# The last turn of a two-layer graph kernel re-ordered, its padding cleared by GpSimd, and the mean of the last normalization taken off by TensorE

## The chip, the core and the metric

The kernel runs on one core of a Trainium2 chip. The metric is device time in microseconds (us), the median of three executions. The core has five engines with a queue each: TensorE (PE in the rows; its weight loads are PEld), VectorE (DVE), ScalarE (ACT), GpSimd (POOL) and SyncE (SP), which here only issues DMAs. They wait for each other by semaphores: an instruction counts one up when it ends, another waits until the count is reached.

## The reference

There are N = 12,500 nodes with D = 32 features and E = 400,000 edges, sorted by destination. Two message layers follow one another, each with a normalization behind it. Cut to what matters:

```
m = relu(x[src] + edge_attr)
x = layernorm(x + (1 + eps) * x + segment_sum(m, dst))

out_deg = clip(segment_sum(1, src), 1);  in_deg = clip(segment_sum(1, dst), 1)
agg = segment_sum((x * rsqrt(out_deg))[src], dst)
x = layernorm(x + agg * rsqrt(in_deg))
```

`layernorm` takes the mean of a node's 32 features off and divides by the square root of the variance plus 1e-5. Everything is float32 (f32).

## The kernel before

**Layer 0** (`layer_0`, lines 221 to 689) goes through the edges in G = 125 groups of 3,200, as 128 partitions by J = 25 edges. Each engine has a function `step(g, slot, u)` that is its share of turn g, and `turns` calls it for g = 0 to 126. In turn g the kernel gathers the feature rows of group g (GpSimd, 25 indirect DMAs, line 163), sums the messages of group g-1, adds what was summed for group g-2 to the accumulator `acc`, and builds counts of group g for layer 1 (TensorE `built`, ScalarE evicts them to `big`, SyncE stores `big` to `stash` in HBM). Turn 125, which the change touches, has no group left to gather or build: it only sums the messages of group 124. Turn 126 only adds the last sums.

What VectorE does for the messages of one group, in halves of 13 and 12 edges: `add(h)` (line 422, waits for the gathered `rows` and for ScalarE's copy of the edge features, L589), `left(h)` (427) and `last_part(h)` (431), between which ScalarE rounds two bf16 parts (596, 600). These three parts of a message go into `msg`. `copy(1)` of ScalarE waits for `last_part(0)`, since both halves use the one bank `sum_ps`. Beside this VectorE makes `indices()` (lines 435 to 440) and from them the one-hots that TensorE multiplies by: `dst_hot`, `hi_hot` and `lo_hot` (all but the last from the helper in line 143, `lo_hot` in line 452). TensorE's 25 matmuls `agg<-hot,msg` (line 663) need all of it: the first 13 wait for the one-hots and the parts of half 0, the other 12 for those of half 1. Once they are done, lines 473 and 474 take the sums out of the bank (`taken`, `degree`).

At the end of layer 0 the buffer `big`, which held counts for `stash`, is used anew: its front becomes `x_0`, the node features. In turn 125 VectorE waits until all stores to `stash` have landed, clears 32 padded partitions (line 470) and counts `z_clear` up. SyncE waits for that and issues the loads of `x_0` (lines 546 and 548).

**finish_0** (lines 1005 to 1173) normalizes after layer 0. It transposes `acc` tile by tile (line 1051), and its first use of `x_0` is line 1060, behind the wait in line 1105. A chain of small DMAs runs beside it: the degrees go to HBM (line 1162) and come back turned (1164, 1165), and line 1114 waits for them. **layer_1** (694 to 900) then multiplies the stored counts by the node table.

**finish_1** (lines 1175 to 1277) is the last stage. The 98 columns of nodes that each partition holds are worked on in 7 chunks of 14 (`FR`), and these in two parts: part 0 has 4 chunks (56 columns, 1,792 elements for each partition), part 1 has 3 (42 columns, 1,344 elements). TensorE turns `acc`, which has features on partitions, into node-major tiles: 98 transposes of 32x128, 14 to a PSUM bank, over four banks. VectorE does `normed(k)` for a chunk (scaling by `r_in`, line 1212), then for a part `mean(h)` (add the residual, reduce, scale: lines 1218, 1220, 1222), `centred(h)` (subtract, 1227), `variance(h)` (1232) and `result(h)` (reciprocal 1237, multiply 1239). ScalarE squares (1259) and takes the root (1261). SyncE stores a part when `result(h)` is done.

`general_sums` is a fallback whose loops are skipped for these inputs; only its branches run. Engines meet at a barrier where one block of the program ends and the next begins.

Of the kernel before, what the change touches and what calls it, by code (L numbers as in the profile page):

```python
# [5 lines left out]
ALU = mybir.AluOpType  # L6
# [3 lines left out]
P = 128  # L10
# [6 lines left out]
def build(nc, x, src, dst, edge, eps, out, table, x1):  # L17
# [47 lines left out]
    with ExitStack() as ctx:  # L65
# [16 lines left out]
        fold = sb("fold", [D3, D])  # L82
        fold_r = sb("fold_r", [R, DE])
# [95 lines left out]
        with nc.Block() as block:  # L179
# [7 lines left out]
            def _(ve):  # L187
# [21 lines left out]
                ve.wait_ge(s_v, n)  # L209
                V(ve.tensor_scalar(fold[:, :], iota[0:D3, 0:D], low[0:D3, 0:1], None, ALU.is_equal))  # L210
# [10 lines left out]
        def layer_0():  # L221
# [37 lines left out]
            with ExitStack() as own:  # L259
# [133 lines left out]
                with nc.Block() as block:  # L393
                    @block.vector
                    def _(ve):
# [16 lines left out]
                        def step(g, slot, u):  # L412
# [47 lines left out]
                            if sends(g):  # L460
                                add(0)
                            if builds(g):
                                chunk(g, k, 1)
                            if sends(g):
                                left(0)
                                indices()
                            if isinstance(g, int) and g == G:
                                for k in range(2):
                                    ve.wait_ge(z_stash[k], (NC + 1 - k) // 2 * 16)
                                ve.memset(x_0[P - 32:P, TAIL:C, :], 0.0).then_inc(z_clear, 1)  # L470
                            if adds(g):
                                ve.wait_ge(z_agg, g - 1)
                                ve.tensor_copy(taken[:, :], agg).then_inc(z_taken, 1)
                                ve.tensor_tensor(degree[:, :], degree[:, :], agg_degree, ALU.add).then_inc(z_degree, 1)
                            if builds(g):
                                chunk(g, k, 2)
                            if sends(g):
                                last_part(0)

                                ve.wait_ge(z_idx, g * 4)  # L480
                                dst_hot(0)
                                add(1)
                                hi_hot(0)
                                left(1)
# [3 lines left out]
                                dst_hot(1)  # L488
                                last_part(1)
                            if adds(g):  # L490
# [61 lines left out]
                    def _(gp):  # L552
# [17 lines left out]
                        turns(gp, step)  # L570

# [603 lines left out]
        def finish_1():  # L1175


            with ExitStack() as own:
# [4 lines left out]
                stat = sb("stat1", [P, C])  # L1183
# [5 lines left out]
                h_stat = sem("h_stat")  # L1189
# [7 lines left out]
                with nc.Block() as block:  # L1197
                    @block.tensor
                    def _(te):
                        for k, (c0, n) in enumerate(FR):  # L1200
                            if k >= 4:
                                te.wait_ge(h_used, k - 3)
                            for t in range(n):
                                last = te.transpose(turn[k % 4][:, t * D:(t + 1) * D], acc[0:D, c0 + t:c0 + t + (P - 1) * C + 1:C], ident[0:D, 0:D])  # L1204
# [3 lines left out]
                    def _(ve):  # L1208
# [6 lines left out]
                        def mean(h):  # L1215
                            c0, c1 = PART[h]
                            ve.wait_ge(h_used, (CUT, len(FR))[h])
                            ve.tensor_tensor(y[:, c0:c1, :], y[:, c0:c1, :], x_n[:, c0:c1, :], ALU.add).then_inc(h_stat, 1)  # L1218
                            ve.wait_ge(h_stat, 3 * h + 1)
                            ve.tensor_reduce(stat[:, c0:c1], y[:, c0:c1, :], AX.X, ALU.add).then_inc(h_stat, 1)  # L1220
                            ve.wait_ge(h_stat, 3 * h + 2)
                            ve.tensor_scalar(stat[:, c0:c1], stat[:, c0:c1], 1.0 / D, None, ALU.mult).then_inc(h_stat, 1)  # L1222

                        def centred(h):
                            c0, c1 = PART[h]
                            ve.wait_ge(h_stat, 3 * h + 3)
                            ve.tensor_tensor(y[:, c0:c1, :], y[:, c0:c1, :], wide(stat, c0, c1), ALU.subtract).then_inc(h_centred, 1)  # L1227
# [15 lines left out]
                        mean(0)  # L1243
                        normed(CUT)
                        centred(0)
                        for k in range(CUT + 1, len(FR)):
                            normed(k)
# [66 lines left out]
```

## Time and profile before

| | us |
|---|---|
| median of 3 runs | 5873.95 |
| lowest, highest | 5873.21, 5877.54 |
| the profiled execution, its own time | 5839.17 |
| its span in the profile | 5837.2 |
| busy TensorE, VectorE, ScalarE, GpSimd | 3442.9, 3286.8, 2727.0, 2960.4 |

Layer 0 ends near 4580 us of the span, finish_0 takes some 37 us more, layer 1 ends near 5800, and finish_1 is the rest. In the rows of a timeline the first number is the start in us from the start of the span, the second the length; then come engine, line, operation, the tiles written and read, their shapes, the count of instructions merged in the row, and in brackets the idle time before it with what ended it. Two such rows of one engine can overlap by about 0.1 us, as one instruction begins while the last drains.

### The profile page before, as it was taken

To read this page: it belongs to the slowest core of one execution; us is meant where nothing else is said; L and a number is where in the kernel's file an instruction comes from. 1 tells how busy PE (TensorE), PEld (TensorE's weight loads), DVE (VectorE), ACT (ScalarE), POOL (GpSimd) and SP (SyncE) were. 2 spreads that over 40 slices of the span, in tenths; PEclk is the share of its full clock that TensorE was granted. 3 is DMA by queue.
4 is the path that set the end of the run, shared out by engine and by line. 5 is a ranking of instruction groups with operands and counts; after the bars stand their busy time and mean duration, and the time that the engine had idled before them with its cause. 6 is when DMAs were issued, how large, how long until landed. Compare 5 with 4: busy or idle time off the path is not lost. (4 is left out here: it accounts for less than half of the span.)

```text
span 5837.2 us, 66492 instructions
## 1 busy us (share of the span) xinstructions
PE 3442.9 (59%) x21147; PEld 1675.5 (29%) x21147; DVE 3286.8 (56%) x4730; ACT 2727.0 (47%) x2908; POOL 2960.4 (51%) x3134
## 2 busy tenths in 40 slices
PE   3445544444444445445445554445444599999997
PEld 1111111111111111111111111111111388888887
DVE  5555555555556556556555555555555544444444
ACT  3444444444444444444444444444444455555553
POOL 4666666666666666666666666666666100000000
PEclk7666666666666666666666666666666699999998
DMA  3333333333233333333333333233333499999996
GB/s 89 105 102 112 106 106 106 106 106 121 95 106 121 101 111 106 106 106 106 106 106 106 106 106 116 96 106 126 103 109 103 150 323 326 325 324 326 323 326 220
DMA packets 273280, 867.72 MB, mean 149 GB/s; under 512 B 94364, under 2 KB 144364, under 8 KB 256748
## 3 DMA queue, kind: packets, MB, share of 16 engines
q1 hardware_dynamic: 173253, 816.00, 37.4%
q0 software_dynamic: 100000, 51.40, 6.3%
q8 instruction: 13, 0.21, 0.0%
q14 instruction: 14, 0.11, 0.0%
HBM read 486.79 MB, written 380.38 MB: 149 GB/s over the span
## 5 line engine op out<-in xcount | busy, mean ns | idle before, releaser
L163 POOL DMA_INDIRECT rows<-in_x,src_t x3125 | 2958.7, 947 | 1589.1 <-issue 914.6
L611 ACT ACTIVATE big<-built 128x980 bf16<-128x980 f32 x1500 | 1797.6, 1228 | 2023.3 <-remote 1624.4
L681 PE MATMUL built<-x_parts,b_hot 100*128 100x490 bf16 x3000 | 1414.7, 572 | 2238.8 <-ACT big L611 1513.0
L681 PEld LDWEIGHTS built<-x_parts,b_hot 100*128 100x128 bf16 x3000 | 242.6, 114 | 3249.1 <-ACT big L611 2084.6
L422 DVE TENSOR_TENSOR sum_ps<-sum_ps,rows 128x416 f32<-128x416 f32 x250 | 143.6, 574 | 1758.5 <-DMA rows<-in_x,src_t 1242.6
L864 PE MATMUL applied<-counts,x_parts 128*96 128x160 bf16 x12250 | 917.2, 233 | 1.4 <-ACT counts L822 1.4
L663 PE MATMUL agg<-hot,msg 128*128 128x512 bf16 x3125 | 908.7, 442 | 5.4 <-DVE msg L452 5.4
L864 PEld LDWEIGHTS applied<-counts,x_parts 128*96 128x96 bf16 x12250 | 881.2, 123 | 65.0 <-ACT counts L822 2.3
L143 DVE TENSOR_TENSOR x_parts<-iota_ps,hk_g 100x3920 bf16<-100x3920 f16 x375 | 820.3, 2187 | 0.0
L822 ACT ACTIVATE counts<-built 128x980 bf16<-128x980 f32 x500 | 598.9, 1239 | 392.0 <-PE built L850 391.9
L143 DVE TENSOR_TENSOR hot<-iota_ps,s_hi 128x5252 bf16<-128x5252 f16 x250 | 692.6, 2770 | 0.0
L663 PEld LDWEIGHTS agg<-hot,msg 128*128 128x128 bf16 x3125 | 353.4, 113 | 513.3 <-issue 254.8
L850 PE MATMUL built<-big,hi_hot 100*128 100x490 bf16 x1000 | 273.3, 374 | 33.6 <-DVE big L143 27.7
L143 DVE TENSOR_TENSOR big<-iota_ps,hk_g 100x3920 bf16<-100x3920 f16 x125 | 273.7, 2190 | 0.0
L143 DVE TENSOR_TENSOR b_hot<-iota_ps,hk_g 100x1024 bf16<-100x1024 f16 x375 | 256.7, 684 | 28.9 <-PE built L681 13.0
L600 ACT ACTIVATE msg<-sum_ps 128x416 bf16<-128x416 f32 x250 | 125.5, 502 | 278.6 <-issue 175.3
L788 DVE CAST slots<-small 80x64 bf16<-80x64 f32 x125 | 27.6, 221 | 374.4 <-PE small L875 374.4
L143 DVE TENSOR_TENSOR hot<-iota_ps,rel 128x1404 bf16<-128x1404 f16 x250 | 211.0, 844 | 0.0
L427 DVE SCALAR_TENSOR_TENSOR sum_ps<-sum_ps,msg 128x416 f32<-128x416 f32 x250 | 142.8, 571 | 45.7 <-ACT msg L596 45.7
L589 ACT ACTIVATE sum_ps<-edge_t 128x416 f32<-128x416 f32 x250 | 126.8, 507 | 85.2 <-issue 52.8
L804 DVE TENSOR_TENSOR acc<-acc,small 32x128 f32 x125 | 34.5, 276 | 206.4 <-PE small L885 206.4
L596 ACT ACTIVATE msg<-sum_ps 128x416 bf16<-128x416 f32 x250 | 122.3, 489 | 43.8 <-DVE sum_ps L422 38.1
(128 smaller groups left out, 1450.2 us busy)
## 6 DMA issues: line engine op xcount, KB each, us to landing
stash<-big SPq DMA_DIRECT2D x125, 2940.0 KB
counts<-stash SPq DMA_DIRECT2D x250, 1470.0 KB, 8.7
rows<-in_x,src_t POOLq DMA_INDIRECT x3125
edge_t<-in_edge_attr SPq DMA_DIRECT2D x61, 800.0 KB
big<-in_dst SPq DMA_DIRECT2D x1, 1562.5 KB
big<-in_src SPq DMA_DIRECT2D x1, 1562.5 KB
src_t<-in_src SPq DMA_DIRECT2D x61, 24.8 KB
dst_t<-in_dst SPq DMA_DIRECT2D x61, 24.8 KB
```

Source lines behind the costliest of these rows:

```text
L143: return ve.tensor_tensor(out.rearrange("p n (w t) -> p n w t", t=2), row[0:p, 0:w].rearrange("p (w t) -> p w t", t=2).unsqueeze(1).to_bro ...
L163: gp.indirect_dma_start(rows_d[:, j, :], None, nodes, bass.IndirectOffsetOnAxis(ap=src_d[:, j:j + 1].bitcast(U32), axis=0),).then_inc(s, 16)
L422: ve.tensor_tensor(half(h), half(h), rows[:, prev, j0:j1, :], ALU.add).then_inc(z_sum, 1)
L427: ve.scalar_tensor_tensor(half(h), half(h), 0.0, part(0, h), ALU.max, ALU.subtract).then_inc(z_left, 1)
L589: sc.activation(half(h), edge_t[:, prev, j0:j1, :], ACT.Copy).then_inc(z_copy, 1)
L600: sc.activation(part(1, h), half(h), ACT.Copy).then_inc(z_part1, 1)
L611: sc.activation(stage[:, slot % 2, q, :, d0:d0 + 2 * SPAN].rearrange("p c (b d) -> p b c d", b=2), built[n % 2][:, :, 0:KEYS].rearrange("p ...
L663: last = te.matmul(agg_bank[:, :], msg[:, j, :], hot[:, j, :], start=(j == 0), stop=(j == J - 1))
L681: last = te.matmul(built[n % 2][:, b, 0:KEYS], b_hot[:, r, t, :], key_hot[:, r, t, :], start=True, stop=True)
L822: sc.activation(counts[:, slot, HB, :, d0:d0 + 2 * SPAN].rearrange("p c (b d) -> p b c d", b=2), built[n % 2][:, :, 0:KEYS].rearrange("p b ...
L850: last = te.matmul(built[n % 2][:, b, 0:KEYS], hi_hot[:, slot, t, :], key_hot[:, slot, t, :], start=True, stop=True)
L864: last = te.matmul(applied[slot].rearrange("m (q d) -> m q d", d=CS), x_parts[:, c, :], counts[:, other, :, c, :], start=(c == 0), stop=(c ...
```

## The change

Three things change.

1. In turn 125 VectorE has an order of its own. It makes the indices, takes out the sums of group 123 (now called `sums_out`), makes all six one-hots, and only then does `add`, `left` and `last_part` of both halves. A new wait, for its own one-hots of the turn before, stands in front. All other turns keep their order.
2. The clearing of the padding leaves VectorE. GpSimd does it when its 125 groups are gathered, behind the same waits for `stash`. SyncE waits for `z_clear` as before.
3. In finish_1 TensorE multiplies by `centre`, the identity less 1/32 in every element, in place of a transpose by the identity. `centre` is symmetric, so a product with it is the transposed tile less its mean over the 32 features. Scaling by `r_in` keeps a mean of zero, and the residual `x_n`, an output of the first normalization, has a mean of zero too, so `mean(h)` loses its reduction and its scaling and the subtraction goes. `centred(h)` is now the addition of the residual. The order of the rest of VectorE's and ScalarE's work changes with it. `centre` is made once at the start of the program.

```
+
+        centre = sb("centre", [D, D])
...
+                V(ve.tensor_scalar(centre[:, :], ident[0:D, 0:D], 1.0 / D, None, ALU.subtract))
...
-                            if sends(g):
-                                add(0)
-                            if builds(g):
-                                chunk(g, k, 1)
-                            if sends(g):
-                                left(0)
-                                indices()
-                            if isinstance(g, int) and g == G:
-                                for k in range(2):
-                                    ve.wait_ge(z_stash[k], (NC + 1 - k) // 2 * 16)
-                                ve.memset(x_0[P - 32:P, TAIL:C, :], 0.0).then_inc(z_clear, 1)
-                            if adds(g):
+                            def sums_out():
                                 ve.wait_ge(z_agg, g - 1)
                                 ve.tensor_copy(taken[:, :], agg).then_inc(z_taken, 1)
                                 ve.tensor_tensor(degree[:, :], degree[:, :], agg_degree, ALU.add).then_inc(z_degree, 1)
-                            if builds(g):
-                                chunk(g, k, 2)
-                            if sends(g):
-                                last_part(0)
-
+                            if isinstance(g, int) and g == G:
+
+                                ve.wait_ge(z_hot, g * 6 - 6)
+                                indices()
+                                sums_out()
                                 ve.wait_ge(z_idx, g * 4)
                                 dst_hot(0)
-                                add(1)
                                 hi_hot(0)
-                                left(1)
                                 lo_hot(0)
                                 hi_hot(1)
                                 lo_hot(1)
                                 dst_hot(1)
+                                add(0)
+                                left(0)
+                                last_part(0)
+                                add(1)
+                                left(1)
                                 last_part(1)
+                            else:
...
+                        for k in range(2):
+                            gp.wait_ge(z_stash[k], (NC + 1 - k) // 2 * 16)
+                        gp.memset(x_0[P - 32:P, TAIL:C, :], 0.0).then_inc(z_clear, 1)
...
-                stat = sb("stat1", [P, C])
...
-                h_stat = sem("h_stat")
...
-                                last = te.transpose(turn[k % 4][:, t * D:(t + 1) * D], acc[0:D, c0 + t:c0 + t + (P - 1) * C + 1:C], ident[0:D, 0:D])
+                                last = te.matmul(turn[k % 4][:, t * D:(t + 1) * D], acc[0:D, c0 + t:c0 + t + (P - 1) * C + 1:C], centre[:, :], start=True, stop=True)
                             last.then_inc(h_turn, 1)
...
-                        def mean(h):
+                        def centred(h):
+
                             c0, c1 = PART[h]
                             ve.wait_ge(h_used, (CUT, len(FR))[h])
-                            ve.tensor_tensor(y[:, c0:c1, :], y[:, c0:c1, :], x_n[:, c0:c1, :], ALU.add).then_inc(h_stat, 1)
-                            ve.wait_ge(h_stat, 3 * h + 1)
-                            ve.tensor_reduce(stat[:, c0:c1], y[:, c0:c1, :], AX.X, ALU.add).then_inc(h_stat, 1)
-                            ve.wait_ge(h_stat, 3 * h + 2)
-                            ve.tensor_scalar(stat[:, c0:c1], stat[:, c0:c1], 1.0 / D, None, ALU.mult).then_inc(h_stat, 1)
-
-                        def centred(h):
-                            c0, c1 = PART[h]
-                            ve.wait_ge(h_stat, 3 * h + 3)
-                            ve.tensor_tensor(y[:, c0:c1, :], y[:, c0:c1, :], wide(stat, c0, c1), ALU.subtract).then_inc(h_centred, 1)
+                            ve.tensor_tensor(y[:, c0:c1, :], y[:, c0:c1, :], x_n[:, c0:c1, :], ALU.add).then_inc(h_centred, 1)
...
                         for k in range(CUT):
                             normed(k)
-                        mean(0)
-                        normed(CUT)
                         centred(0)
-                        for k in range(CUT + 1, len(FR)):
+                        for k in range(CUT, len(FR)):
                             normed(k)
+                        centred(1)
                         variance(0)
-                        mean(1)
                         result(0)
-                        centred(1)
                         variance(1)
                         result(1)
 
                     @block.scalar
                     def _(sc):
-                        for h, (c0, c1) in enumerate(PART):
+                        def squares(h):
+                            c0, c1 = PART[h]
                             sc.wait_ge(h_centred, h + 1)
                             sc.activation(sq[:, c0:c1, :], y[:, c0:c1, :], ACT.Square).then_inc(h_squares, 1)
+
+                        def deviation(h):
+                            c0, c1 = PART[h]
                             sc.wait_ge(h_var, h + 1)
                             sc.activation(rstd[:, c0:c1], var[:, c0:c1], ACT.Sqrt, bias=ln_eps[:, 0:1], scale=1.0 / D).then_inc(h_dev, 1)
+
+                        squares(0)
+                        squares(1)
+                        deviation(0)
```

VectorE in turn 125, before. The first row is `add(0)`; `hot` and the rows of L452 are the one-hots:

```order
L422 TENSOR_TENSOR sum_ps<-sum_ps,rows 128x416
L427 SCALAR_TENSOR_TENSOR sum_ps<-sum_ps,msg 128x416
L435 TENSOR_TENSOR rel<-dst_t,base_all 128x50
L436 TENSOR_SCALAR quot<-src_t 128x25
L438 TENSOR_SCALAR s_hi<-quot 128x50
L440 SCALAR_TENSOR_TENSOR s_lo<-s_hi,src_t 128x50
L470 MEMSET big 32x1408
L473 COPY taken<-agg 128x108
L474 TENSOR_TENSOR degree<-degree,agg 32x404
L431 TENSOR_TENSOR msg<-sum_ps,msg 128x13x32
L143 TENSOR_TENSOR hot<-iota_ps,rel 128x13x108
L422 TENSOR_TENSOR sum_ps<-sum_ps,rows 128x384
```

The same place after, from the removal of the sums on:

```order
L465 COPY taken<-agg 128x108
L466 TENSOR_TENSOR degree<-degree,agg 32x404
L145 TENSOR_TENSOR hot<-iota_ps,rel 128x13x108
L145 TENSOR_TENSOR hot<-iota_ps,s_hi 128x13x404
L455 TENSOR_TENSOR msg<-iota_ps,s_lo 128x13x31
L145 TENSOR_TENSOR hot<-iota_ps,s_hi 128x12x404
L455 TENSOR_TENSOR msg<-iota_ps,s_lo 128x12x31
L145 TENSOR_TENSOR hot<-iota_ps,rel 128x12x108
L425 TENSOR_TENSOR sum_ps<-sum_ps,rows 128x416
L430 SCALAR_TENSOR_TENSOR sum_ps<-sum_ps,msg 128x416
L434 TENSOR_TENSOR msg<-sum_ps,msg 128x13x32
L425 TENSOR_TENSOR sum_ps<-sum_ps,rows 128x384
```

The memset is gone from this queue, and the six one-hots stand in one block ahead of the additions.

VectorE in finish_1, before, from the fourth chunk's end on:

```order
L1218 TENSOR_TENSOR y<-y,big 128x1792
L1220 TENSOR_REDUCE stat<-y 128x56
L1222 TENSOR_SCALAR stat<-stat 128x56
L1212 TENSOR_TENSOR y<-turn,r_in 128x448
L1227 TENSOR_TENSOR y<-y,stat 128x1792
L1212 TENSOR_TENSOR y<-turn,r_in 128x448 x2
L1232 TENSOR_REDUCE var<-sq 128x56
L1218 TENSOR_TENSOR y<-y,big 128x1344
L1220 TENSOR_REDUCE stat<-y 128x42
L1222 TENSOR_SCALAR stat<-stat 128x42
L1237 RECIPROCAL rstd<-rstd 128x56
L1239 TENSOR_TENSOR big<-y,rstd 128x1792
```

The same after, to the end of the program:

```order
L1233 TENSOR_TENSOR y<-turn,r_in 128x448 x4
L1240 TENSOR_TENSOR y<-y,big 128x1792
L1233 TENSOR_TENSOR y<-turn,r_in 128x448 x3
L1240 TENSOR_TENSOR y<-y,big 128x1344
L1245 TENSOR_REDUCE var<-sq 128x56
L1250 RECIPROCAL rstd<-rstd 128x56
L1252 TENSOR_TENSOR big<-y,rstd 128x1792
L1245 TENSOR_REDUCE var<-sq 128x42
L1250 RECIPROCAL rstd<-rstd 128x42
L1252 TENSOR_TENSOR big<-y,rstd 128x1344
```

All work on part 0 behind its addition now comes after the last of the seven chunks. On TensorE the stage has one row in both programs, 98 products of 128x32, with `ident` before and with `centre` after.

## Rows read from the trace of the kernel before

**Rows 1.** Timeline of VectorE, turns 124 to 126 and finish_0's start.

```profile
4541.65 0.26 DVE L495 TENSOR_REDUCE counted<-fold_bank 1x1 f32<-1x108 f32 x1
4555.03 0.60 DVE L422 TENSOR_TENSOR sum_ps<-sum_ps,rows 128x416 f32<-128x416 f32 x1 [13.12 <-issue]
...
4563.27 1.23 DVE L470 MEMSET big<- 32x1408 f32 x1 [4.32 <-DMA stash<-big]
...
4565.70 0.87 DVE L143 TENSOR_TENSOR hot<-iota_ps,rel 128x1404 bf16<-128x1404 f16 x1
...
4574.49 0.54 DVE L431 TENSOR_TENSOR msg<-sum_ps,msg 128x384 bf16<-128x384 f32 x1
...
4583.11 0.15 DVE L1106 TENSOR_SCALAR eps_t<-eps_t 128x1 f32<-128x1 f32 x1
```

**Rows 2.** Timeline of TensorE, the agg matmuls of groups 123 and 124.

```profile
4543.41 4.26 PE L663 MATMUL agg<-hot,msg 128*128 128x512 bf16 x19
...
4570.84 7.16 PE L663 MATMUL agg<-hot,msg 128*128 128x512 bf16 x25 [5.41 <-DVE msg L452]
```

**Rows 3.** Timeline of ScalarE in turn 125.

```profile
4558.17 0.52 ACT L600 ACTIVATE msg<-sum_ps 128x416 bf16<-128x416 f32 x1 [0.67 <-DVE sum_ps L427]
```

**Rows 4.** Timeline of SyncE's queue at the end of layer 0.

```profile
4564.60 0.82 SPq L546 DMA_DIRECT2D big<-in_x  x2
...
4583.11 0.28 SPq L1162 DMA_DIRECT2D degree_d<-degree_t  x1
4590.88 0.22 SPq L1164 DMA_DIRECT2D r_out<-degree_d  x1
```

**Rows 5.** GpSimd's largest fill, from the program's start.

```profile
L184 POOL IOTA x_parts<- x1: 532/532/532, 1.1 to 1.1; 128x490 int32 x1
```

**Rows 6.** Stretches: busy of PE, PEld, DVE, ACT, POOL; PEclk; DMA share; GB/s.

```profile
4570.00:4572.00 2.00, 1.16 (x3) 0.44 (x4) 2.00 (x3) 0.49 (x1) 0.00 (x0) 0.50 0.92 198
4581.80:4582.80 1.00, 0.90 (x5) 0.87 (x6) 0.15 (x2) 0.00 (x0) 0.00 (x0) 0.50 0.07 16
5788.90:5789.40 0.50, 0.50 (x11) 0.50 (x10) 0.03 (x1) 0.00 (x0) 0.00 (x0) 1.00 0.00 0
5802.30:5814.10 11.80, 11.78 (x98) 11.66 (x98) 6.72 (x8) 0.00 (x0) 0.00 (x0) 0.50 0.01 3
```

**Rows 7.** Timelines of TensorE: three streams of small f32 products.

```profile
5802.31 11.78 PE L1204 MATMUL turn<-ident,acc 32*128 32x32 f32 x98 [2.98 <-PEq L914]
...
4581.90 0.85 PE L1045 MATMUL fold_bank<-ident,degree 32*101 32x32 f32 x4 [3.17 <-PEq L914]
...
5788.86 0.36 PEld L875 LDWEIGHTS small<-fold,prod 96*80 96x80 f32 x4
```

**Rows 8.** Weight loads by line: ns min/median/max, first and last start, form.

```profile
L380 PEld LDWEIGHTS built<-base_f,ones_row x2: 283/306/328, 78.1 to 78.3; 1*128 1x128 f32 x2
...
L1204 PEld LDWEIGHTS turn<-ident,acc x98: 189/210/212, 5802.3 to 5813.7; 32*128 32x128 f32 x98
```

**Rows 9.** The chain that ended last, in finish_1: start, length, what.

```profile
5809.15 0.64 DVE y L1212
...
5811.87 2.03 DVE stat L1220
...
5818.34 2.02 DVE var L1232
5820.36 1.48 DVE y L1218
...
5824.08 2.03 DVE big L1239
...
5828.96 1.56 DVE var L1232
...
5830.91 0.43 DVE rstd L1237
...
5831.36 1.56 DVE big L1239
```

## What is predicted

> **What bounds the kernel now.** The change touches two short stretches, so I read those, not the shares of the page. First VectorE's timeline at the end of layer 0, to see what it waits for and who waits for it [rows 1 to 3]; then SyncE's queue there, since the end of `big`'s old use releases loads [rows 4]; then the chain that ended last in finish_1, and what TensorE does in it [rows 6, 7, 9].
>
> In turn 125 VectorE is idle from 4541.9 us, when it has added the sums of group 122, to 4555.03, when the gathered rows and the copied edge features are there [rows 1]. Then it makes the additions and stops until the last store to `stash` has landed, at 4563.27, clears the padding for 1.23 us, and only from 4565.70 on makes one-hots. The last part of the messages starts at 4574.49. TensorE's 25 matmuls wait for that queue: they start at 4570.84 and end at 4578.0 [rows 2], and all of finish_0 stands behind them. The 13 idle us and the wait for the store are both on the path.
>
> In finish_1 TensorE is the feeder at first: 98 transposes in 11.78 us from T = 5802.31, one each 0.12 us [rows 7]. VectorE starts the residual of part 0 after the fourth chunk, at T + 7.5, and from there on VectorE (with ScalarE's squares) is the path, to 5831.36 + 1.56 = 5832.92, T + 30.6 [rows 9]. The transposes of part 1 are hidden behind part 0.
>
> **Part 1, the order of turn 125.** The new wait on `z_hot` is for VectorE's own older work and costs nothing. The wait for group 123's sums now stands ahead of the one-hots and the additions: TensorE is done with them at 4543.41 + 4.26 = 4547.67 [rows 2]. Taking them out costs some 0.75 us, to 4548.4. The one-hots took, before, from 4565.70 to 4574.49, 8.8 us, in which one `add` and one `left` stand, about 0.5 us each in the queue: 7.85 us alone. They end at 4548.4 + 7.85 = 4556.3, which is 1.3 us after the rows were there, so the rows don't limit. Then the two halves are a serial chain between VectorE and ScalarE, with ScalarE's steps 0.52 us [rows 3] and VectorE's 0.6 [rows 1]: add 0.64, relu 0.56, left 0.64, second part 0.56, last part 0.61 gives 4559.3, where TensorE may start. Half 1 needs six such steps, 3.3 us, to 4562.6; TensorE by then has not finished the 13 matmuls of half 0 (25 take 7.16 us, the first of them the slowest), so it doesn't stop. Start 4559.3 in place of 4570.84 is **11.5 us** earlier, and 7.16 us of matmuls end at 4566.5.
>
> **Part 2, the padding.** The store lands at 4563.27 as before, since nothing ahead of it moves. GpSimd is done with its gathers by then, and its only late duty is the clearing; what is behind it in its queue is the barrier alone. VectorE took 1.23 us. No row shows GpSimd clearing 1,408 elements; its fill of 490 took 0.53 us [rows 5], so 1,408 are at most 1.53 us, and it could be as quick as VectorE. I take 1.4: SyncE issues the loads of `x_0` 0.2 us later than 4564.60 [rows 4]. Behind them the DMA engines were busy until 4572 [rows 6]. Before, `x_0` had 11 us to spare: the wait in line 1105 lies at 4583.11 [rows 1]. Now that point moves to 4571.6 and the loads end at 4572.2: the cover is used up. VectorE's next step waits for TensorE anyhow, so 0.6 us there is made good. But `degree_d` is stored at the same moment, on the same queue, and its trip out takes 7.77 us (4583.11 to 4590.88) [rows 4]; line 1114 of VectorE waited 0.46 us for what comes of it. Whatever the tail of `x_0` costs that chain goes to the end of finish_0. I take 0.5 us, bounds 0 and 2.3 (the loads end at 4573.9 and all of that counts). Layer 0 and finish_0 together: 11.5 - 0.5 = **11.0 us gained**, 9 to 11.5. Layer 1 just starts earlier.
>
> **Part 3, the products with `centre`.** Making `centre` is one small instruction in the first 4 us, before VectorE waits for the first indices: nothing. What goes is reductions, scalings and subtractions of VectorE, as the 2.03 us of L1220 for part 0 [rows 9]. What comes is hidden in a word of the diff: a transpose is one pass, a product of two f32 operands is two. In `x4` for the two products of L875 and `x2` for the one of L380 it can be read, against `x98` for 98 transposes [rows 7, 8]. So 196 passes take the place of 98.
>
> And a pass is slower. The transposes of 128 columns run 0.118 us apart, (11.78 - 0.30) / 97. The passes of ordinary f32 products load their weights at another rate: the four loads of 80 columns in L875 lie (0.36 - 0.15) / 3 = 0.070 us apart with the granted clock at 1.00, so 0.140 at 0.50, which is 1.75 ns a column and 0.224 us for 128 [rows 6, 7]. L1045, at 0.50, is a transpose of 101 columns and goes slower than that of 128: (0.85 - 0.35) / 3 = 0.167 us, 1.65 ns a column, 0.212 us for 128 [rows 6, 7]. The only ordinary f32 load of 128 columns, L380, lasts 283 and 328 ns where L1204's last 189 and 210 [rows 8]: it belongs to the slow kind. So the pass costs 0.118 at least, 0.224 plus 0.05 for its product if nothing overlaps, and I take 0.215. [...] 196 x 0.215 = 42.1 us, 42.3 with the last one's end.
>
> Now TensorE is the path to the last chunk, at T + 42.3. Part 0's residual and squares are long done, but its variance stands behind part 1's residual in VectorE's queue. From there: scaling 0.64, residual of part 1 1.48, variance 2.02, root 0.39, reciprocal 0.45, multiply 2.03, variance 1.56, root 0.39, reciprocal 0.45, multiply 1.56 [rows 9]: 11.0 us, to T + 53.3. Before it was T + 30.6: **22.7 us lost**. With 0.212 to 0.224 it is 22.1 to 24.5. The store behind it is the same.
>
> **Sum.** -11.0 + 22.7 = +11.7 us. The profiled execution's own 5839.17 would be 5850.9. The median of the runs is 34.8 us above that execution, in both kernels I assume, so 5873.95 + 11.7 = **5885.6**. The bounds of the terms alone give +10.6 to +15.5; with 2 us for the spread of the runs, 5882 to 5890.
>
> A measurement of this kernel can tell about 0.2%, 11.75 us, from no change. The forecast lies on that line: slower by just under 0.2%.
>
> **Rivals.** *A: the loads are as quick as those of the transposes.* 128 columns with 0.118 us between two would make 196 x 0.118 = 23.1 us, 19.0 less than in my sum: finish_1 loses 3.7, the whole is -7.3 us, 5866.7. Against it stand the durations of L380, for it that 128 columns were quicker than 101 among the transposes. It decides from 0.155 a pass down, where the whole is a gain. [...] Chance 0.12.
>
> *B: the clock rises.* The new passes compute where the old ones only moved data. With the granted clock at 1.00 a pass is 0.112 us (0.224 / 2). If it rises some 4 us into the stage (a guess; each us later costs 0.5), the stage of TensorE is 19 passes in 4.1 us and 177 in 19.8: 23.9 us, 18.2 less, the whole -6.5 us, 5867.5. Against it: TensorE's records are busy 11.78 of 11.80 us and the clock stayed at 0.50 [rows 6], and the new products come at longer distances than the transposes, not shorter. [...] Chance 0.14.
>
> *A and B at once*: 12 us of TensorE, VectorE is the path, and the subtractions saved come out as a gain of 6 us or so; the whole -17, 5857. Chance 0.02.
>
> *C: the cover of the end of layer 0 is thinner.* GpSimd's clearing at 4 ns an element is 5.6 us; `x_0` then lands at 4576.4, 4.8 us after line 1105 needs it, and the gain is 6.7: +16, 5890. It costs from 0.6 us on, one for one. The same time comes if the weight load and the product of a pass don't overlap in part (0.24 us). Chance 0.08. L875 shows overlap.
>
> **How the numbers follow.** My forecast has 0.64, and half of it lies beyond 0.2%. Slower by over 0.2%: 0.32 + 0.08 = 0.40. Faster by over 0.2%: 0.02, and 0.02 for more gain in A or B. Within 0.2%: 0.32, A and B with 0.24: 0.56. The likeliest case alone holds 5882 to 5890; to leave out no more than 2 in 10 the range goes down to A and B: 5866 to 5890.
>
> **What would show it.** Of finish_1: the row of TensorE's products with x196 and 42 us long at a granted clock of 0.50; 23 us long with 0.50 is A, with 1.00 in the later part B. VectorE waits for TensorE ahead of each of the seven chunks, about 5 us each. Of layer 0: one-hots from about 4548.4 on without a memset among them, TensorE's 25 matmuls at 4559.3, line 1105 near 4571.6; a longer wait ahead of it is C. If rows come after 4556, the gain of part 1 is smaller by that. The prediction is wrong if TensorE's stage is shorter than 36 us or longer than 46.

## The result, and the profile after

The changed kernel takes 5906.1 us, median of 5 runs (5902.75 to 5907.71), against 5875.15 us for the kernel before in runs beside it (5873.21 to 5877.54): ratio 1.0052, 95% interval 1.0042 to 1.0063. That is 31.0 us slower, where 11.7 were forecast, and above the range of 5866 to 5890 us. On a second chip the same pair gave 1.0052 again (1.0038 to 1.0066, 29.7 us). The profiled execution of after took 5907.56 us, its span is 5905.6.

The chain that ended last, in finish_1, in order of time (start, length, what); it answers to [rows 9]:

```profile
5842.52 47.84 PE turn L1225 x196
...
5890.39 0.64 DVE y L1233
...
5891.05 1.56 DVE y L1240
5892.60 1.94 DVE var L1245
...
5895.48 2.02 DVE big L1252
5897.51 1.47 DVE var L1245
...
5899.82 1.56 DVE big L1252
```

TensorE alone is the path for 47.84 us, and behind it stand 11.0 us of VectorE and ScalarE. The stage ends at 5901.38, T + 58.9, where before ended at T + 30.6: **28.3 us** more. The timelines of TensorE and of VectorE there, and the row of the stretch (busy PE, PEld, DVE, ACT, POOL; granted clock; DMA share; GB/s), which answer to [rows 6, 7]:

```profile
5842.52 47.83 PE L1225 MATMUL turn<-centre,acc 32*128 32x32 f32 x196 [2.99 <-PEq L937]
```

```profile
5849.55 0.62 DVE L1233 TENSOR_TENSOR y<-turn,r_in 128x448 f32<-128x448 f32 x1 [9.60 <-PE turn L1225]
5856.35 0.62 DVE L1233 TENSOR_TENSOR y<-turn,r_in 128x448 f32<-128x448 f32 x1 [6.18 <-PE turn L1225]
```

```profile
5842.50:5890.40 47.90, 47.83 (x196) 47.72 (x196) 5.78 (x8) 1.70 (x1) 0.00 (x0) 0.50 0.00 1
```

196 passes as forecast, but 47.83 / 196 = 0.244 us each where 0.215 stood in the sum, at a granted clock of 0.50 to the last. VectorE works 0.62 us and waits 6.18 for the next chunk.

Now turn 125. GpSimd's last gather and its clearing, TensorE's products for groups 123 and 124, VectorE's removal of the sums, its first one-hot and its first addition; they answer to [rows 1, 2]:

```profile
4593.65 0.95 POOL L165 DMA_INDIRECT rows<-in_x,src_t  x1 [0.30 <-issue]
4605.13 1.27 POOL L593 MEMSET big<- 32x1408 f32 x1 [10.53 <-DMA stash<-big]
```

```profile
4582.81 4.26 PE L686 MATMUL agg<-hot,msg 128*128 128x512 bf16 x19
...
4610.65 8.44 PE L686 MATMUL agg<-hot,msg 128*128 128x512 bf16 x24 [10.68 <-DVE msg L434]
```

```profile
4582.37 0.27 DVE L443 SCALAR_TENSOR_TENSOR s_lo<-s_hi,src_t 128x50 f16<-128x50 f16 x1
4599.07 0.27 DVE L465 COPY taken<-agg 128x108 f32<-128x108 f32 x1 [16.43 <-remote]
...
4599.74 0.87 DVE L145 TENSOR_TENSOR hot<-iota_ps,rel 128x1404 bf16<-128x1404 f16 x1
...
4607.61 0.58 DVE L425 TENSOR_TENSOR sum_ps<-sum_ps,rows 128x416 f32<-128x416 f32 x1
```

The order is the new one, but it starts late. TensorE's products of group 123 end at 4582.81 + 4.26 = 4587.07 in its records, and VectorE, idle from 4582.6 on, copies them only at 4599.07, 12.0 us later and 4.5 us after the last gather ends (4594.60). By the code that copy waits for one count, `z_agg`, which the last of those products raises. Everything else then stands in a row: 7.9 us of one-hots, 3.0 us of additions, products at 4610.65. "remote" says that the profile found no releaser beside it.

To compare turns of different kernels I need a common mark, since profiles of one kernel differ by up to 37 us in when the gathers end, even where the times of the two chips differ by 4 us (4552.74 in the first profile of before, 4590.03 in the third). I use the **last gather's end**: how much later the products into `agg` for group 124 start, and how much of the span is left. Before: 4570.84 - 4552.74 = 18.1 us and 1284.5 us left; after: 16.05 and 1311.0. The rest grew by 26.5: 28.3 of finish_1 less 1.8.

### The profile page after: what moved, and what is told of

The parts are those of the page before. It is cut to its first block and busy times, and to the rows that moved or that the text cites. A ratio compares the mean times of both kernels' runs of the same rounds, so it can differ in the third digit from the quotient of the medians.

```text
span 5905.6 us, 66559 instructions
## 1 busy us (share of the span) xinstructions
PE 3465.1 (59%) x21120; PEld 1710.1 (29%) x21245; DVE 3280.9 (56%) x4724; ACT 2731.2 (46%) x2908; POOL 2969.6 (50%) x3135
## 5 line engine op out<-in xcount | busy, mean ns | idle before, releaser
L686 PE MATMUL agg<-hot,msg 128*128 128x512 bf16 x3000 | 859.6, 435 | 38.0 <-issue 27.2
```

Of the source, the lines that this page charges most:

```text
L686: last = te.matmul(agg_bank[:, :], msg[:, j, :], hot[:, j, :], start=(j == 0), stop=(j == J - 1))
```

## The experiments

Three chips were used, the first for the first four kernels, the second for the next four, the third for the rest. The medians of the kernel before on them are 5233.89, 5862.47 and 5870.99 us. So each edit is compared with before on its own chip, and each difference below is one of medians.

**The kernel before again.** No edit.

> The kernel before, unchanged, to see a second profiled execution of it. The first took 5839.17 us by its own count where five timed runs of the same kernel have a median of 5875.15, and in it the last gather of layer 0 ended at 4552.74, in the profile of the changed kernel at 4594.60. Theory 1: the 42 us between the two belong to that one execution and not to the change. Then this profile's own time lies within 5870 to 5880 and its last gather ends between 4585 and 4595. Theory 2: the changed kernel has a longer layer-0 loop. Then the last gather ends within 5 us of 4553 here too. In either case finish_1 takes 30.6 us from TensorE's first transpose to the last multiplication, and TensorE's 25 matmuls of turn 125 start 18 us after the last gather ends.

5233.69 us: neither theory, as the chip is another. finish_1 took 30.6 us as expected; the 18 us to the products were a miss. Its last gather, VectorE's first addition and clearing, and the products for group 124:

```profile
3952.67 0.94 POOL L163 DMA_INDIRECT rows<-in_x,src_t  x1 [0.31 <-issue]
```

```profile
3955.11 0.60 DVE L422 TENSOR_TENSOR sum_ps<-sum_ps,rows 128x416 f32<-128x416 f32 x1 [12.76 <-DMA rows<-in_x,src_t]
...
3958.06 1.23 DVE L470 MEMSET big<- 32x1408 f32 x1 [0.35 <-issue]
```

```profile
3965.63 7.80 PE L663 MATMUL agg<-hot,msg 128*128 128x512 bf16 x24 [5.42 <-DVE msg L452]
```

Products 12.0 us after the last gather instead of 18.1: the 4.3 us that [rows 1] shows as a wait for `stash` are 0.35 here, and no engine waits for TensorE's count.

**finish_1 alone.** Before, with `centre` and the changed finish_1:

```
-  te.transpose(turn[k % 4][...], acc[...], ident[0:D, 0:D])
+  te.matmul(turn[k % 4][...], acc[...], centre[:, :], start=True, stop=True)
   (and VectorE's and ScalarE's order of the change)
```

> The kernel before with the change in finish_1 alone (product with centre, no mean). Theory 1, the loss is all here: TensorE's 196 passes take 47.8 us as in the changed kernel (0.244 us each at a granted clock of 0.50), finish_1 takes 58.9 us in place of 30.6, and the time is 28.3 us above the kernel before, 5903. Theory 2, a part of the loss is in the layer-0 loop or its end: the time is less than 25 us above. By my prediction's own term it would be +22.7.

5262.42 us, ratio 1.0054 (1.0041 to 1.0068): 28.5 us slower.

```profile
5197.69 47.82 PE L1204 MATMUL turn<-centre,acc 32*128 32x32 f32 x196 [2.98 <-PEq L916]
```

The same row and the same price on another chip, as the first theory expected (28.3). finish_1 alone is worth the whole loss there.

**Turn 125 alone.** The changed kernel, with finish_1 of before and no `centre`.

> The kernel before with turn 125's order and GpSimd's clearing alone; finish_1 is that of before. By my prediction: 11 us quicker. Theory 1, the signal that the sums of group 123 are done reaches VectorE late (12 us after TensorE's last such matmul by the records of the changed kernel), so that the one-hots can't start in the idle time: 2 us quicker, 0 to 4, with the sums taken out some 4 to 5 us after the last gather ended. Theory 2, the changed code also makes the layer-0 loop longer: 2 to 6 us slower than before.

5226.88 us, ratio 0.9987 (0.9978 to 0.9996): 7.0 us faster. TensorE and VectorE:

```profile
3944.44 4.26 PE L684 MATMUL agg<-hot,msg 128*128 128x512 bf16 x19
...
3960.31 7.60 PE L684 MATMUL agg<-hot,msg 128*128 128x512 bf16 x24 [10.87 <-DVE msg L432]
```

```profile
3948.74 0.27 DVE L463 COPY taken<-agg 128x108 f32<-128x108 f32 x1 [4.61 <-PE agg L684]
```

Here the sums are taken 0.04 us after TensorE has made them, while GpSimd still gathers (to 3954.78). The one-hots lie beside the last gathers, and the products start 5.5 us after them. 12.0 - 5.5 = 6.5 of the 7.0 us. The 2 us of the first theory were a miss: on this chip the signal is not late.

**The mean folded in earlier, and the transposes back.** The sums of `acc` in layer 1 pass through a product with a constant matrix `fold` in any case, so the mean can be taken off there, by other constants in the same product:

```
-  ve.tensor_scalar(fold[:, :], iota[0:D3, 0:D], low[0:D3, 0:1], None, ALU.is_equal)
+  ve.tensor_scalar(fold[:, :], iota[0:D3, 0:D], low[0:D3, 0:1], 1.0 / D, ALU.is_equal, ALU.subtract)
-  te.matmul(turn[k % 4][...], acc[...], centre[:, :], start=True, stop=True)
+  te.transpose(turn[k % 4][...], acc[...], ident[0:D, 0:D])
```

> The changed kernel, but the mean is taken off earlier: the matrix fold, which layer 1 multiplies its sums by in any case (32 moving columns), has 1/32 taken from every element when it is made, so the sums come centred out of a product that is there anyway, and finish_1 goes back to 98 transposes by the identity with the reductions still gone. The fallback path, which these inputs don't take, would need the mean taken off as well. Theory 1: TensorE's stage takes 11.8 us again, finish_1 is bound by VectorE and takes about 23 us (last scaling at T + 12.1, then 11.0), 7.5 less than before; with the 2 us of turn 125 the time is about 9.5 us under the kernel before, 5866. If the passes were not what costs finish_1 its time, it would stay near 59 us.

5219.81 us, ratio 0.9972 (0.9961 to 0.9982): 14.1 us faster than before. TensorE's row and VectorE's last one:

```profile
5191.73 11.79 PE L1223 MATMUL turn<-ident,acc 32*128 32x32 f32 x98 [3.00 <-PEq L935]
```

```profile
5212.97 1.56 DVE L1250 TENSOR_TENSOR big<-y,rstd 128x1344 f32<-128x1344 f32 x1
```

The stage ends at T + 22.8, 7.8 us sooner than before. With 7.0 from turn 125 that makes 14.8, against 14.1 measured.

**The same products from contiguous columns.** The changed kernel, with one operand read otherwise; the sums land at wrong nodes.

```
-  acc[0:D, c0 + t:c0 + t + (P - 1) * C + 1:C]
+  acc[0:D, (c0 + t) * P:(c0 + t + 1) * P]
```

> The changed kernel with one operand read elsewhere: the stationary 32x128 block of acc in finish_1 is taken as 128 neighbouring columns in place of every 98th, so nodes come out in the wrong places; as many passes, as many columns, the same waits. Theory 1, the stride of 392 bytes is what makes a pass dearer than the 0.212 to 0.224 us that I had scaled from contiguous loads: the 196 passes take 42 to 44 us, 0.215 to 0.224 each. Theory 2, a load of 128 f32 columns costs 0.244 us however it lies, and the scaling by columns was wrong: 47.8 us again.

One execution, profiled, on a chip of 5862 us: 5885.56 us. TensorE's row:

```profile
5826.36 41.99 PE L1225 MATMUL turn<-centre,acc 32*128 32x32 f32 x196 [2.99 <-PEq L937]
```

41.99 us, 0.214 a pass, against 47.83 with a step of 98 elements (392 bytes): the step costs 0.030 us a pass, 5.8 in all. The 42.1 of the forecast was right for contiguous columns. The loads say the same: 328 ns in the median here, as the longer one of L380 in [rows 8], and 336 ns with the step:

```profile
L1225 PEld LDWEIGHTS turn<-centre,acc x196: 283/328/328, 5826.3 to 5867.9; 32*128 32x128 f32 x196
```

**Turn 124 with one gather.** The changed kernel; of the 25 gathers for group 124 only the first is made, so that GpSimd is idle while TensorE finishes group 123. The other rows keep values of an older group, so the sums are wrong; the run is for its profile.

```
-  gathers(gp, 0, J, ...)
+  gathers(gp, 0, 1 if isinstance(g, int) and g == G - 1 else J, ...)
   (and the wait for the rows counts as many)
```

> The changed kernel, but of the last group (124) only one of the 25 gathers is made, the other 24 rows keep what a group before left there, and VectorE waits for as many fewer. The time is some 30 us less for that alone. In the profile of the changed kernel the sums of group 123 were done on TensorE at 4587.07 and VectorE took them out only at 4599.07, 4.5 us after the last gather; in another execution set (the kernel with turn 125's order alone) there was no such delay. Theory 1, the gathers that run beside TensorE hold its signals back where the delay exists: with them gone VectorE takes the sums within 1 us of TensorE's end. Theory 2, the delay has another source: it stays near 12 us. If this chip shows no delay in the whole kernel either (gathers of two turns 0.3 us apart and not 5), the run tells nothing on that.

GpSimd's one gather, TensorE's products for group 123 and VectorE's copy of them:

```profile
4551.87 0.94 POOL L165 DMA_INDIRECT rows<-in_x,src_t  x1 [5.29 <-remote]
```

```profile
4569.53 4.54 PE L686 MATMUL agg<-hot,msg 128*128 128x512 bf16 x19
```

```profile
4574.10 0.27 DVE L465 COPY taken<-agg 128x108 f32<-128x108 f32 x1 [5.29 <-PE agg L686]
```

4569.53 + 4.54 = 4574.07, and the copy follows 0.03 us later, with TensorE named as its releaser. Without the gathers the 12 us of lateness are gone: on this kind of chip the gathers that run beside TensorE hold its signal back. By what path, no run shows. The time, 5881.76 us, is 10.4 less than that of the changed kernel on this chip; the 30 us that were expected for the missing gathers were a miss, as TensorE's products for group 123 now end after them.

**The clearing alone moved.** Before, with the wait for `stash` and the memset in GpSimd's queue behind its turns.

```
-  ve.wait_ge(z_stash[k], (NC + 1 - k) // 2 * 16)
-  ve.memset(x_0[P - 32:P, TAIL:C, :], 0.0).then_inc(z_clear, 1)
+  gp.wait_ge(z_stash[k], (NC + 1 - k) // 2 * 16)
+  gp.memset(x_0[P - 32:P, TAIL:C, :], 0.0).then_inc(z_clear, 1)
```

> The kernel before with only the clearing of the padding moved to GpSimd; VectorE's order in turn 125 stays, less the memset and its wait. Theory 1, where the store to stash lands early (as in the second profile of the kernel before, where the wait ahead of the memset was 0.35 us), only the 1.23 us of the memset and 0.4 us of wait go: 1.6 us quicker, and the rest of the 7.0 us that both layer-0 edits gave is the order's. Theory 2, the clearing's place is what gives most of it: 5 us or more. On a chip where the store lands late (4.3 us of wait, as in the first profile of before) theory 1 gives 5.5 us.

5861.41 us, ratio 0.9998 (0.9989 to 1.0007): no difference that can be measured, and too wide an interval (6.4 us faster to 4.1 slower) to tell 1.6 us from 5. In its profile, 4.5 us after the last gather (4576.92) ScalarE gets what it waits for, the same signal of TensorE:

```profile
4581.47 0.52 ACT L595 ACTIVATE msg<-sum_ps 128x416 bf16<-128x416 f32 x1 [11.14 <-remote]
```

```profile
4589.65 7.38 PE L662 MATMUL agg<-hot,msg 128*128 128x512 bf16 x24 [5.41 <-DVE msg L452]
```

The products start 12.7 us after the last gather, 3.3 us sooner than in the changed order. In the order of before only the three one-hots of half 0 stand ahead of the first product (0.87 + 2.87 + 0.55 us in its rows), and half 0's additions are made before them; in the changed order all six, 7.9 us, stand ahead of any addition.

**The changed kernel again.** No edit.

> The changed kernel, unchanged, beside the kernel before on this chip. If the parts add up (finish_1 alone +28.5, turn 125 alone -7.0, both measured on the chip where two gathers of different turns lie 0.3 us apart), it is 21.5 us slower than before. On a chip like that of the first comparison, where the gathers of two turns lie 5 us apart and the time before is 5875, it is 31 us slower again, as turn 125 gives 2 us or nothing there.

5892.16 us, +29.7: the second case, 31, and not the 21.5 of the first chip's parts. The last gather ends at 4579.07, and:

```profile
4583.45 0.27 DVE L465 COPY taken<-agg 128x108 f32<-128x108 f32 x1 [18.38 <-remote]
```

4.4 us after it again; the products at 4595.02, 16.0 after it.

**The kernel before, a third time**, on a third chip.

> The kernel before, profiled once more for its turn 125. If this chip is one on which the gathers of neighbouring turns lie about 5 us apart (5862 to 5875 us), the theory (VectorE learns of group 123's aggregate some 4.4 us after the last gather, and the one-hots of before are made beside that) expects the products into agg for group 124 to begin 12 to 14 us after the last gather ends, and the 18.1 us of the first profile to be an outlier; the rival (18.1 us is the rule, so the change did save 2 us there) expects 17 to 19. If it is a chip of 5234 us both expect 12.

A miss: the products start at 4607.17, 17.1 us after the last gather, not 12 to 14; so far the rival's 17 to 19. The cause is not the one of the first profile. There the clearing waited 4.3 us for `stash`; here the gathered rows themselves are late, and the wait for `stash` is gone:

```profile
4589.08 0.95 POOL L163 DMA_INDIRECT rows<-in_x,src_t  x1 [0.30 <-issue]
```

```profile
4596.65 0.60 DVE L422 TENSOR_TENSOR sum_ps<-sum_ps,rows 128x416 f32<-128x416 f32 x1 [18.62 <-DMA rows<-in_x,src_t]
...
4599.60 1.23 DVE L470 MEMSET big<- 32x1408 f32 x1 [0.35 <-issue]
```

So the order of before is exposed to two transfers, the rows and the store, and with either one late its products start 17 to 18 us after the last gather. In the changed order they start 15.8 to 16.1 us after it in all five profiles on such chips, also where the store lands 10.5 us after the last gather, as in the first (GpSimd's memset above).

**Turn 125 alone, on the third chip.**

> The changed turn 125 (one-hots early, clearing on GpSimd) with the finish_1 of before. Theory (what turn 125 gains hangs on how late the signals of TensorE come to VectorE while GpSimd gathers): on a chip of 5862 to 5875 us between -1 and +2 us, on one of 5234 us -7 again. Rival (the edit is worth 6 to 11 us on any chip, and finish_1 costs more than its row says): -6 to -11 on both.

5872.47 us, ratio 0.9999 (0.9990 to 1.0008), +1.5 us, as the theory expected. The last gather ends at 4588.93, and:

```profile
4593.38 0.27 DVE L463 COPY taken<-agg 128x108 f32<-128x108 f32 x1 [15.66 <-remote]
```

The sums are taken 4.45 us after the last gather, and the products start 16.0 us after it. The same program that gained 7.0 us on the chip of 5234 us gains nothing that can be measured here.

**The order of before, the clearing on GpSimd, the mean in `fold`.** The edits of the clearing alone and of the mean folded in earlier, together, on before.

> The order of before in turn 125 with the clearing alone moved to GpSimd, and finish_1 with the mean taken off inside the fold matrix, the turn of the nodes staying a transpose. Theory: 7.1 to 7.8 us less in finish_1 and 1.1 us less in turn 125, so -8 to -9 on a chip of 5862 us. Rival (the early one-hots are needed for a gain): -7 or less, below the next kernel.

5860.94 us, ratio 0.9983 (0.9974 to 0.9992): 10.0 us faster than before, where 8 to 9 were expected.

**The mean in `fold`, with the changed turn 125, on the third chip.**

> The changed kernel with finish_1's products against centre turned back into transposes, the mean taken off inside the fold matrix. Theory: on a chip of 5862 to 5875 us -6 to -7 (7.1 to 7.8 less in finish_1, about 1 more in turn 125), on one of 5234 us -14 again. Rival (the early one-hots are worth as much everywhere): -14 on both.

5863.98 us, ratio 0.9988 (0.9979 to 0.9997): 7.0 us faster, as the theory expected. Both of the last two beat both kernels; the intervals don't separate them. On the chip of 5234 us the second gained 14.1, and the first wasn't run there.

The profiles side by side. "Rest" is the span less the last gather's end, the column "finish_1" has that stage from T (the start of TensorE's products in it) to its end, and "less finish_1" takes it off the rest, and so shows the turn, finish_0 and layer 1 alone:

| kernel, turn 125 | chip us | agg after the last gather | rest | finish_1 | less finish_1 |
|---|---|---|---|---|---|
| before | 5874 | 18.1 | 1284.5 | 30.6 | 1253.9 |
| before, third | 5871 | 17.1 | 1282.7 | 30.6 | 1252.1 |
| clearing alone | 5862 | 12.7 | 1278.2 | 30.6 | 1247.6 |
| clearing and fold | 5871 | 12.5 | 1271.4 | 22.8 | 1248.6 |
| after | 5875 | 16.0 | 1311.0 | 58.9 | 1252.1 |
| after again | 5862 | 16.0 | 1309.6 | 58.9 | 1250.7 |
| turn 125 alone | 5871 | 16.0 | 1282.8 | 30.6 | 1252.2 |
| changed turn and fold | 5871 | 15.8 | 1274.0 | 22.8 | 1251.2 |
| contiguous columns | 5862 | 15.9 | 1303.8 | 53.0 | 1250.8 |
| before, again | 5234 | 12.0 | 1278.1 | 30.6 | 1247.5 |
| finish_1 alone | 5234 | 12.1 | 1306.2 | 58.9 | 1247.3 |
| turn 125 alone | 5234 | 5.5 | 1271.1 | 30.6 | 1240.5 |
| changed turn and fold | 5234 | 6.5 | 1265.0 | 22.8 | 1242.2 |

The last column gives the new order 5 to 7 us on the chip of 5234 us and, on the others, about 1.6 us: 1253.0 in the mean of two profiles with the order of before, 1251.4 in the mean of five with the changed one. The times there say +1.5 and, after finish_1's 28.3 is taken off, +2.7 and +1.4: nothing either way, as the end of the gathers moves by more than that from run to run.

By the same column the clearing alone is worth more on these chips than the whole new order, 4.4 to 5.4 us. Its times say 1.1 us and, after the 7.8 of `fold` is taken off, 2.2. The two profiles of before each had one late transfer; whether most executions have one, and so which order is the better there, stays open.

## Why the prediction was wrong

**What held.** The 98 products left 196 records of a pass, two for each product as in L875 (x4 for two) and L380 (x2 for one), where the 98 transposes left 98 [rows 7, 8]. The clock, which the sum kept at the 0.50 of the transposes [rows 6], was granted at 0.50 to the end; what follows the last chunk took 11.0 us as forecast. The sign of the sum and the share of finish_1 as its largest part were right.

**Part 3, the price of a pass.** This step failed: a pass was priced at 0.215 us and took 0.244, and TensorE's stage took 47.8 us, beyond the 46 that I had named as the sign of being wrong. I had scaled the price from loads of 80 columns (L875) and of 101. It is the contiguous price, 0.214 measured, and that it fits so well is in part luck, since the row of 101 columns is a transpose. The load of 80 columns was read at a granted clock of 1.00 and doubled for 0.50; that factor was an estimate, as L875 has no row at 0.50. The bf16 products of L864 have rows at both in the trace of before: 24 take 3.41 us from 4640.49 on at 0.50, 0.142 each, and 41 take 3.02 us from 5789.17 on at 1.00, 0.074 each, a factor of 1.9. The operand here steps over 98 elements, and its passes take 0.244. The transposes read the same step at 0.118, so nothing suggested that the step costs; but no strided f32 product was among my rows, and the upper end should have stood further out than 0.224. The term was +22.7 and is +28.3: 5.6 us of the miss. The other upper bound, another 0.05 for a product that doesn't overlap, would have held it; I left it beside rival C, at 0.24.

**Part 1, the start of the new order.** I let VectorE take the sums at the end of TensorE's record, 4547.67, "some 0.75 us, to 4548.4". The step that failed is that VectorE hears of it then. The profile of before had shown it: in [rows 3] a neighbouring ScalarE step, and beside it this wait of ScalarE for the same count, with the last gather ended at 4552.74:

```profile
4556.98 0.52 ACT L596 ACTIVATE msg<-sum_ps 128x416 bf16<-128x416 f32 x1 [2.06 <-remote]
```

It runs 9.3 us after TensorE's record ends, 4.2 us after the last gather. On the chips of 5862 us and more there are eight profiles of the full gathers in which VectorE or ScalarE waits for this count and nothing later; in all eight it gets it 4.2 to 4.6 us after the last gather. So there the one-hots don't lie beside the gathers, and the new order puts 7.9 us of them in front of the additions, where the order of before had them between. It is paid back by the waits for `rows` and `stash` that it hides. The term of layer 0 and finish_0 was -11.0 and is about -1.6 there by the profiles, and not clear of nothing by the times: some 9 us of the miss. On the chip of 5234 us, where the signal comes at once, the start of the products 5.5 us after the last gather agrees with the forecast's 4559.3 - 4552.74 = 6.6; the gain is 7.0 and not 11.5 there since before starts its products after 12.0 us and not 18.1: it has no wait for `stash` to lose, and its ScalarE doesn't wait for TensorE's count.

**Part 2.** GpSimd's memset took 1.27 us, against 1.4 taken and 1.53 as the bound. The trip of `degree_d` was 7.73 us (4624.07 to 4631.80), against 7.77 in [rows 4], and no wait for `x_0` appeared: the 0.5 us of cost was not there.

With the measured terms the sum is -1.6 + 28.3 = +26.7 us; the runs say 29.7 and 31.0. Both intervals of these, 22.3 to 38.7 and 24.7 to 37.0 us, hold the 26.7, so the 3 to 4 us between need no cause, and no run shows one.

**The rivals.** *A* (loads as quick as a transpose's): refuted, 0.244 and even contiguous 0.214, against 0.118. A load of the products lasts 336 ns in the median, 328 with contiguous columns, and one of the transposes 210 [rows 8]. For the same 98 tiles the products took 47.83 us and the transposes 11.78, a ratio of 4.1; with contiguous columns it is 41.99 / 11.78 = 3.6. *B* (the clock rises): refuted, the granted clock was 0.50 over 47.9 us in which TensorE is busy 47.83. It does rise elsewhere: in a stretch of before in which TensorE is busy from 4627.95 on, it is 0.50 until 4632.00 and 1.00 from 4632.25. Why it stayed at 0.50 in finish_1, no run shows. *C* (a thinner cover, GpSimd slow): its own mechanism did not occur: GpSimd's memset of 1,408 elements took 1.27 us, 0.9 ns an element, where this rival had 4. The pass of 0.24 us that I named beside it did, but not for the reason given there: the step makes it, as contiguous columns are at 0.214.

## What to carry to other kernels

When a transpose on TensorE is replaced by a product "that does the arithmetic on the way", count and price the passes from rows of such products. Here the 98 transposes (x98, 0.118 us apart) became 196 passes (x196) of 0.214 us with contiguous columns, 1.8 times as long, and of 0.244 us with the step of 392 bytes in the stationary operand. Look first for a product that is made anyway, as the one with `fold` here, and change its constants. And when work is moved to lie beside other engines' work, ask when its engine *hears* of what it waits for, from a row of that wait, not from the end of the producer's record.

## What the hardware showed that I had not expected

- While GpSimd issues indirect gathers, a count of TensorE reaches VectorE and ScalarE 9 to 14 us late in eight profiles on chips of 5862 to 5875 us, and within 0.04 us in two profiles on the chip of 5234 us. Whether DMA traffic, GpSimd's instruction or the count itself is held was not told apart.
- The same program differs by 640 us between chips, and most of it is layer 0. The last gather ends at 3953.6 and at 4590.0 in two profiles of the kernel before. On the slow ones GpSimd waits about 5 us before the gathers of a turn. These are all its gathers in the first and in the second profile of before (busy, mean ns; idle before them, and what ended it):

```profile
L163 POOL DMA_INDIRECT rows<-in_x,src_t x3125 | 2958.7, 947 | 1589.1 <-issue 914.6 <-remote 623.2 <-PE agg L663 46.8
L163 POOL DMA_INDIRECT rows<-in_x,src_t x3125 | 2959.1, 947 | 989.6 <-issue 948.7 <-PE agg L663 36.1 <-DMA dst_t<-in_dst 4.8
```

  The idle time differs by 599.5 us, and the last gather's end by 599.1 (4552.74 and 3953.61). The 623.2 us of "remote" are 122 waits, 5.1 us each, and are missing on the fast chip. GpSimd too waits for `z_agg` there, so it is likely the same late count that makes these chips 12% slower; that the count is what it waits for longest is argued from the code and not shown.
- The stationary operand of the f32 products in finish_1 costs 0.030 us more a pass with a step of 392 bytes (0.244 us) than without (0.214); the transposes of the same operand, with that step, are 0.118 us apart.
